# Splitting GpSimd's four row scatters of a loop body into two pairs, one of them behind the residual add

## What is computed

```python
x = x + layernorm(attention(layernorm(x)))   # gated linear attention, 16 heads of 16
x = x + layernorm(ffn(layernorm(x)))         # 8 experts, each token uses its best 2, and a shared expert

# attention: q = elu(x Wq * s)+1, k = elu(x Wk)+1, v = x Wv, gate g = sigmoid(x Wg + bg)
#   S_t = g_t * S_(t-1) + k_t v_t^T ;  y_t = q_t S_t ;  out = y Wo
# ffn: swiglu(x, w1, w2, w3) = (h * sigmoid(h) * (x w2)) w3 with h = x w1
#   out = sum over the chosen 2 experts of softmax weight * swiglu_e(x) + swiglu_shared(x)
```

## Time and profile before

| | before |
|---|---|
| median of 3 runs | 885.7 us (880.39, 885.7, 886.43) |
| the profiled execution, its own time | 884.06 us |
| its span | 881.7 us |
| PE busy | 779.2 us (88%) |
| DVE busy | 559.7 us (63%) |
| ACT busy | 423.7 us (48%) |
| POOL busy | 413.8 us (47%) |
| the 64 scatters on POOL (L544) | 94.3 us, mean 1473 ns |

### The profile page before, as it was taken

How to read it: one execution, slowest core, us unless ns; L and a number is a source line. 1 busy time by engine, 2 the same in 40 slices (tenths; PEclk the granted TensorE clock), 3 DMA queues, 4 the chain that set the end, 5 groups by cost and what they waited for, 6 DMA issues and landing times.

```text
span 881.7 us, 24476 instructions
## 1 busy us (share of the span) xinstructions
PE 779.2 (88%) x8205; PEld 551.0 (62%) x8205; DVE 559.7 (63%) x1195; ACT 423.7 (48%) x811; POOL 413.8 (47%) x452
## 2 busy tenths in 40 slices
PE   3879888898999984899999999999999999977772
PEld 3667667687877763466666666666666666644441
DVE  4797988897988993699433334433334433477774
ACT  2555556565666552343444444444444444444442
POOL 3122335876777775681899960000000000377773
PEclk8899989999999997799999999999999999999996
DMA  7243333443345347781111111111111212345554
GB/s 238 68 102 83 98 101 78 141 121 110 111 138 144 111 121 264 271 287 48 44 60 56 62 58 58 61 58 59 60 55 61 61 60 63 96 131 186 168 156 130
DMA packets 71381, 96.55 MB, mean 109 GB/s; under 512 B 8800, under 2 KB 58080, under 8 KB 71264
## 3 DMA queue, kind: packets, MB, share of 16 engines
q1 hardware_dynamic: 59376, 69.31, 26.5%
q0 software_dynamic: 6528, 17.83, 6.2%
q10 hardware_dynamic: 5360, 7.87, 2.7%
HBM read 63.25 MB, written 31.72 MB: 108 GB/s over the span
## 4 chain that ended last, share of the span: by engine, by line
PE 44%; DMA 5%; DVE 4%; issue 4%; POOL 3%; ACT 0%; POOLq 0%; SPq 0%; ACTq 0%; DVEq 0%
PE bank L1208 25%; PE bank L1218 12%; DMA ya<-ys_scratch,gi 4%; PE bank L1199 4%; PE bank L1193 2%; POOL ya L1475 2%; DVE cmb L1367 1%; DVE cmb L1373 1%; DVE stc L1378 0%; POOL xs_scratch L544 0%; DVE mvc L1384 0%; DMA xt<-xs_scratch 0%; POOL rsc L1481 0%; DVE vec L1387 0%; PE bank L741 0%
## 5 line engine op out<-in xcount | busy, mean ns | idle before, releaser
L1208 PE MATMUL bank<-W,xh 128*128 (+1 forms) x832 | 249.4, 382 | 15.3 <-DVE xl L1414 15.1
L1407 DVE TENSOR_TENSOR gl<-bank,gh 128x512 f16<-128x512 f32 x104 | 71.7, 690 | 162.9 <-ACT gh L1258 162.8
L1208 PE MATMUL bank<-W,xl 128*128 (+1 forms) x416 | 158.5, 381 | 0.0
L1218 PE MATMUL bank<-W,gh 128*128 (+1 forms) x832 | 143.4, 274 | 0.0
L1208 PEld LDWEIGHTS bank<-W,xh 128*128 128x128 f16 x832 | 80.4, 98 | 73.6 <-DVE xl L1414 19.7
L1218 PE MATMUL bank<-W,gl 128*128 (+1 forms) x416 | 114.1, 274 | 0.0
L1425 DVE SCALAR_TENSOR_TENSOR gg<-sl,w_scale,bank 128x512 f32<-128x512 f32 x104 | 77.6, 747 | 56.1 <-PE bank L1208 52.1
L1469 POOL COPY gi<-pos_all 128x4 uint32 (+1 forms) x16 | 2.9, 179 | 232.4 <-DMA ys_scratch<-yo 232.4
L544 POOL DMA_INDIRECT xs_scratch<-xn,posi x64 | 94.3, 1473 | 31.8 <-issue 23.2
L1218 PEld LDWEIGHTS bank<-W,gh 128*128 128x128 f16 x832 | 81.9, 98 | 31.8
L600 PE MATMUL bank<-xnT,wT 128*128 128x256 f32 x384 | 94.8, 399 | 0.7 <-ACT xnT L386 0.7
(11 more groups left out here) (177 smaller groups left out, 1325.8 us busy)
## 6 DMA issues: line engine op xcount, KB each, us to landing
W<-gate_scratch SPq DMA_DIRECT2D x64, 256.0 KB, 4.8
xt<-xs_scratch SPq DMA_DIRECT2D x104, 128.0 KB, 2.0
ys_scratch<-yo SPq DMA_DIRECT2D x72, 128.0 KB, 1.7
W<-in_L_ffn_ew_dram ACTq DMA_DIRECT2D x15, 512.0 KB, 6.3
W<-in_L_ffn_ew_dram SPq DMA_DIRECT2D x9, 512.0 KB, 8.3
x_in<-in_L_attn_x_dram SPq DMA_DIRECT2D x16, 256.0 KB, 4.0
x_scratch<-x SPq DMA_DIRECT2D x16, 256.0 KB, 2.2
xs_scratch<-xn SPq DMA_DIRECT2D x16, 256.0 KB, 3.1
```

The costliest lines, as they stand in the source:

```text
L1208: last = mm(dst[t.side][:, :], a[t.side][:, k, :], W16[:, e, m, s, k * H:(k + 1) * H], start=(n == 0), stop=(n == 3 * KC - 1))
L1218: last = mm(pYB[t.side][:, 0:D], a[t.side][:, c, :], W16[:, e, 2, s, c * D:(c + 1) * D], start=(n == 0), stop=(n == 3 * HC - 1))
L1407: V.tensor_tensor(gl[u.side][:, :, :].rearrange("p c t -> p (c t)"), pGT[:, :], gh[u.side][:, :, :].rearrange("p c t -> p (c t)"), ALU.sub ...
```

## The change

The function `scatter` issued all four indirect DMAs of a step. Now it takes the sequence b and issues the two of that sequence. The two of sequence 0 stay where the four were. The two of sequence 1 stand behind the residual, as the last of POOL's body. Numbers, sizes and buffers of the DMAs are the same, and so is every other instruction.

```diff
-            def scatter(s):
+            def scatter(s, b):
                 need(pool, S["pos_ready"], s // BATCH + 1)
                 need(pool, S["xn2_ready"], B * (s + 1))
-                for b in range(B):
-                    for k in range(TOPK):
-                        settle(pool)
-                        pool.indirect_dma_start(
+                for k in range(TOPK):
+                    settle(pool)
+                    pool.indirect_dma_start(
...
                 on(rstd_x, i)
                 on(rstd_x1, i - 3)
-                on(scatter, i - XB)
+                on(lambda s: scatter(s, 0), i - XB)
                 on(rstd_o, i - 2)
                 on(gated_q, i - 1)
                 on(residual, i - 2)
+                on(lambda s: scatter(s, 1), i - XB)
```

More of the change, by code:

```diff
@@ L536, in rstd_x1 @@
                 rstd(rs2, sh2, mv2, 2, s, "x1_stats", "rstd2_ready", "xn2_ready")
-            def scatter(s):
+            def scatter(s, b):
                 need(pool, S["pos_ready"], s // BATCH + 1)
                 need(pool, S["xn2_ready"], B * (s + 1))
-                for b in range(B):
-                    for k in range(TOPK):
-                        settle(pool)
-                        pool.indirect_dma_start(
-                            xs_d[:, :], bass.IndirectOffsetOnAxis(
-                                ap=posi[:, s, b * TOPK + k:b * TOPK + k + 1], axis=0),
-                            xn2[s % XB][:, b, :], None).then_inc(scattered[s % XB], 16)
+                for k in range(TOPK):
+                    settle(pool)
+                    pool.indirect_dma_start(
+                        xs_d[:, :], bass.IndirectOffsetOnAxis(
+                            ap=posi[:, s, b * TOPK + k:b * TOPK + k + 1], axis=0),
+                        xn2[s % XB][:, b, :], None).then_inc(scattered[s % XB], 16)
             def gated_q(s):
```

## The result

| | before | after |
|---|---|---|
| median of 22 runs each | 879.75 us (872.06 to 888.08) | 885.88 us (877.84 to 894.81) |
| ratio after / before | | 1.0085, 95% interval 1.0059 to 1.0111 |
| profiled execution, its own time | 884.06 us | 890.12 us |
| its span | 881.7 us | 888.4 us |
| the 64 scatters on POOL | 94.3 us | 80.5 us, mean 1258 ns |

The kernel became slower by 0.85%, which is 7.5 us of the median before. Ratios in this document leave out the executions that took over 1.5% longer than the fastest of the same kernel, so they differ a little from the quotient of the medians, and the profiled executions of only_even and after_again are among those left out. The forecast was a ratio of 889.3 / 885.7 = 1.0041. The direction, the place and the first step were right; in this comparison the size came out at about twice the forecast.

The account below looks back on a forecast made before the run. PE was taken to bound the first stage, DVE just behind. 2.4 us in the bodies plus 1.2 at the stage's end made 3.6, so 885.7 became 889.3 us; range of 8 in 10: 880 to 902.

Parts of the forecast that it names:

- The bound and the path: First stage: PE bounds, DVE just behind; POOL counts only by when its small results are ready, against PE's slack.
- The pair's price: Behind the residual on POOL: the moved pair takes 2.78 us ahead of rx and rx1, its scatters undisturbed at 0.96 us.
- stretched pair: Slower rival: the pair takes 5.07 us behind the residual; total 904.4 us, chance 0.18 for 893 to 905.
- rival of DVE held by the scatters: Each scatter holds DVE's short state-update instructions up to 0.96 us, 17 us over nine bodies; about 903 us, chance 0.07.
- from rx to PE: Bodies 9 and 11 to 15: late rx delays ACT and PE's transpose; 4.3 us raw, 2.4 after covered parts.
- The even bodies: PE's stalls from late rx: 0.2 us in body 12, 0.8 in 14; nothing in 8 and 10, slack over 5 us.
- The covers: Existing PE waits, 1.43 us before body 14's update and 0.67 in body 15, swallow 1.2 and most of 0.8 us.
- The load and the clock: DVE's 7.9 us of waits for the gates' load change by at most 3 us; 1 us stalls don't lower the clock.
- faster case: Rival: moving a pair off the rush halves DVE's waits for the gates' load, -4 us; total 880.6 us, chance 0.20.
- The freed place: Where the moved pair stood: rstd_o starts about 1.1 us earlier in five bodies; nothing further counted as gain.
- The end: Stage's end, body 17: rx1 starts 1.2 us later, and this goes whole to the start of the second stage.

Follow-up runs that it names:

- only_even: Changed kernel, but the second pair stands behind the residual only in even bodies, in odd ones ahead of rstd_o; 923.08 us, ratio 1.0150 to the kernel before.
- after_again: The changed kernel run once more, unaltered, beside the kernel before; 885.03 us, ratio 1.0033 (0.9984 to 1.0081).
- before_again: The kernel before run once more, unaltered, as a second profile of it; 879.95 us, ratio 1.0009 against itself.
- pair_mid: Changed kernel with the second pair between rstd_o and gated_q, ahead of the residual; 889.0 us, ratio 1.0149 to the kernel before.
- four_behind: Kernel before with all four scatters moved behind the residual; 957.36 us, ratio 1.0901 to the kernel before.
- after_nops: Changed kernel with 128 empty instructions ahead of PE's first one; 887.86 us, ratio 1.0085 to the kernel before.
- one_behind: Three scatters ahead of rstd_o, only the last behind the residual, where the changed kernel has two; 915.78 us, ratio 1.0101 to the kernel before.
- old_tail: Changed kernel up to body 15; from body 16 on the four scatters stand together where they were; 884.33 us, ratio 1.0109 to the kernel before.
- rx_first: Changed kernel with rx of the next body moved ahead of the second pair; 890.79 us, ratio 1.0165 to the kernel before.

## Why the prediction was right

- **The bound and the path.** Right: PE's slack ahead of the transpose of xn2 was what counted. New stalls stand at L731 behind ACT, and at no other wait for POOL's results.
- **The pair's price.** 2.78 us forecast, 2.5 measured; the gap behind the residual is 0.17 us and not 0.56. The stretched pair, my slower rival, did not come: 1.08 and 0.96 us. Nor did the rival of DVE held by the scatters. sdec and state took 10.6 and 9.8 us for 20 each, 9.7 and 8.1 before, and 8.6 and 7.8 in after_again, 8.6 and 8.7 in before_again. The 2.6 us more in the first pair of profiles come from rows of over 1.2 us, nine in place of six, all of them beside residuals; beside the scatters these instructions took 0.28 to 0.32 us. Only a copy of 0.18 us took 0.41 beside a scatter, twice. That the rule behind this rival isn't empty, though, pair_mid shows: there a scatter held gz.
- **The mis-sized term is "from rx to PE".** I moved rx and rx1 by the pair's length and kept their own durations. From before's trace I had that a scatter can't finish while a scan runs, and I applied it to scatters only. (As a rule it is too wide: in four_behind a scatter issued at 220.39, ahead of the scan that began at 220.97, ended at 221.35 in the middle of it.) In body 9 norm_x1 ended at 193.97 + 1.09 = 195.06, and PE stalled 1.98 us where I had 0.95 (192.1 - 191.18 is 0.92). Some 0.3 us of the difference came by rx: 0.5 for its held instruction less 0.3 for the shorter pair. The other 0.7 is a wait that I had at nothing: norm_x1 stood 0.66 us for rx1, whose held instruction took 1.4 us more, and mask_q hid only the first part of that. In 11, 13 and 15 it was 0.79, 1.29 and 1.10 for 1.05, 1.2 and 0.1, and in after_again 0.79, 0.88 and nothing.
- **The even bodies.** 0.2 and 0.8 us forecast for 12 and 14, nothing measured at L731: the stall inside attend, which I had counted as slack for 8 and 10 only, came there too (1.71 and 3.07 us at L704; 1.70 and 0.53 in after_again).
- **The covers.** Neither is in the profile after, so there more of the raw sum reached the time. They come and go: the one ahead of body 14's update was 1.43 and 0.94 us in the two profiles before, absent in after_again and 1.26 in after_nops, and body 15's was 0.67, 0.87, 0.58 and 0.84.
- **The load and the clock.** DVE's waits for the gates went from 7.9 to 5.3 us, and from 9.3 to 10.1 in the second pair of profiles, under the 3 us that I had set down, so the faster case didn't come. After the new stalls of 0.79 to 1.98 us the granted clock was 1.00 (195 to 200, 235 to 240, 270 to 275 and 310 to 315 us), as in the forecast.
- **The freed place.** Right that rstd_o is in time and that this is worth nothing: POOL now waits for ln_o at the residual in nine bodies, 14.4 us in all.
- **The end.** 1.2 us forecast; the distance from the residual to rx1 grew from 2.52 to 3.83 us, 1.3, of which 0.1 came back by rstd_o. Between the transposes of bodies 17 and 18 the profiles differ by 0.8 us.

From residual to residual, body 7 to body 17, the profile grew from 341.44 - 161.26 = 180.18 us to 347.67 - 163.62 = 184.05: 3.9 us. In the second pair of profiles it is 346.1 - 161.4 = 184.7 against 337.0 - 154.0 = 183.0: 1.7. But the two profiles of the kernel before differ by 2.8 us over the same bodies, and one_behind (183.5) and old_tail (183.4) lie as near to the one as to the changed kernel. The profiles' own times differ by 6.06 us, of which 2.4 lie ahead of the first scatter, where nothing was changed. The traced steps thus agree with a loss of the forecast's size and can't fix it closer. The 7.5 us of the first comparison has a part that I can't place; the second one, 1.0033, is under the forecast.

That the sum came near is in part luck. In the first profile body 9 was 1.0 us over its term, body 15 another 1.0, and the covers of 1.9 us failed, while bodies 12 and 14 gave nothing for their 1.0 us; and the holding of small instructions, which made the largest stall, wasn't in the sum at all.

## What to carry to other kernels

When a block moves in an in-order queue, check for everything queued behind it not only how much later it comes, but what the neighbour engine runs at its new time. On GpSimd an instruction of 0.2 us on two numbers per partition cost up to 2.0 us more beside a VectorE scan of 2.3 us, and the result of such an instruction may be what another engine waits for; the scatters that the same scans had stretched showed no cost on PE's path in this stage.

A slack read from one profile is good for its size, but a cover (another stall that happens to swallow the new one) isn't to be relied on: the one of 1.43 us here was 0.94, 0 or 1.26 us in other profiles.

## What the runs showed that I had not expected

- Some instructions of GpSimd and of VectorE exclude each other: in the changed kernel and in rx_first scans held `ve`, `nm` and `sh` (0.2 us) so that they took up to 2.1 us; in pair_mid GpSimd's gated_q and residual held VectorE's `state` (0.29 us), which took up to 1.93 us, and a scatter held gz (0.41 us), which took up to 1.03 us. The Trainium skill (SBUF — State Buffer, the section on the two physically separate sides) says that the one that starts first has the shared port pair for its whole length. The rows of the scans and of gz agree; in pair_mid, though, the residual started 0.52 us behind `state` and ran its usual 1.26 us, and `state` ended 0.14 us behind it.
- Doubling the moved scatters cost ten times as much (1.0901 for 1.0085). From the residual of body 7 to that of body 17 four_behind took 247.95 us, 67.8 more than before; 42.3 us of this are stalls at L731 (43.2 against 0.9). The granted clock was 0.86 between 200 and 250 us, behind stalls of up to 7 us; how the rest divides isn't shown.
- PE's stalls of up to 3.7 us inside attend stand at the same matmuls in most profiles, change their length from one to the next, and did not move with 128 instructions put ahead of them.
